# Step 0's order on TensorE, the keys' lower halves, and a block finished ahead of a maximum, in a fused attention and gated-mix block on one core

## The chip, the cores and the metric

One core of a Trainium2 chip runs the whole program; the other cores are idle. The time is the device time of one execution in microseconds. Before the change it is the median of three runs. One more execution was profiled, and all views below are of that one.

## What is computed

Inputs: `x` of 64 blocks with 256 rows and 512 columns, a context of the same shape, a 512 x 512 output weight with its bias, three 512 x 512 weights `W_r`, `W_k`, `W_v`, mixing vectors `mu_r`, `mu_k`, and two gates. All is float32. For each of the 64 blocks:

```python
q  = relu(layernorm(x)) per head (16 heads of 32)
k  = v = relu(ctx)      per head
att = softmax(q @ k.T / sqrt(32))            # 256 x 256 for each head
z  = relu((att @ v) @ ffn_w.T + ffn_b)
x1 = x + tanh(g_xattn) * z
xn = layernorm(x1); xp = xn shifted down by one row
r  = sigmoid((mu_r*xn + (1-mu_r)*xp) @ W_r)
kk = square(relu((mu_k*xn + (1-mu_k)*xp) @ W_k))
out = x1 + tanh(g_ffn) * r * (kk @ W_v)
```

## The kernel before

**A pipeline over the blocks.** `pipeline` (line 207) runs `iteration(i)` for i from -2 to 66; each of the five instruction streams (SP, POOL, ACT, VectorE, TensorE) has its own `iteration` with its own order written out by hand, and semaphores tie them together. No planner moves anything: every engine runs its list in order, and a wait holds all that stands behind it on that engine. The middle iterations are a hardware loop over pairs. In iteration i TensorE works on four blocks at once: the attention of block i, the first scores of block i + 1, the output projection of block i - 1, and the three products of the second half for block i - 2. The 16 steps of an iteration are separated by `shifted_scores(i, n)` for n from 0 to 15.

**Attention.** A product in high accuracy is three products of high and lower halves. Keys and queries are stacked instead: three groups of 32 rows (high, high, low halves) make one product with 96 rows. `scores(b, n)` (897) gives the scores of head n; `head_max` (692, VectorE) takes their maxima by rows; after four heads `turn_m` (879) transposes the maxima, `copy_m` (703) copies them to `m_t`, and `move_m` on SP's queue brings them as a 97th row beside the stacked queries. `shifted_scores` (910) makes the scores anew, transposed and with the maximum taken off; `exponent` on ACT makes `probs`. For each group of four heads c, `values(b, c)` (922) and `denominators(b, c)` multiply `probs` by the values and by ones, both in 32-column pieces into one bank. `norm_o(b, c)` (710, VectorE) divides. It waits for the denominators and for the landing of the previous group's `write_o`.

**From attention to the projection.** `write_o(b, c)` (282) puts a group, 128 KB, of `o_val` into DRAM, `read_o(b, u)` (288) reads two groups back transposed when both have landed; `o_high` on ACT (499) and `o_low` on POOL (359) split them, and `project(b, u, part)` (955) multiplies them with the weight. Its part 0 first puts the bias into the bank by a product with ones (line 960), then waits for `o_hi` and `o_lo`.

**The dense products.** `dense(q, part)` on TensorE stands for a quarter of one product into one bank: q 0 and 1 are `key` for block i - 2, 2 and 3 `project` for block i - 1, 4 and 5 `receptance`, 6 and 7 `value`, both for block i - 2. `finish(b, u)` (765, VectorE) waits for `value` and makes the output rows; its first instruction frees the bank that `dense(0, 0)` or `dense(1, 0)` of the next iteration takes.

**Transposes.** `turn(n)` takes the nth entry of a list of 14 transposes of queries, maxima or `xn`. All write one bank, so each waits until the one before is copied out.

**Keys.** SP loads `k_raw` of block i + 2 (`load_k`, 246) once block i + 1's keys are written. ACT makes the high halves (`k_halve`, 481), VectorE the lower ones in place (`k_low`, 679), SP writes both, 1 MB, to DRAM (`write_k`, 253), and `stack_k` (266) reads them back into the stacked form, one group of heads at a time. Before the change `k_halve(i + 2)` stands behind exponent 10, `k_low(i + 2)` is the last entry of VectorE's iteration behind `head_max(i + 1, 6)`, and `write_k(i + 2)` the last of SP's, behind `write_o(i, 2)`.

**Step 0 before.** On TensorE the order is `dense(0, 0)`, `scores(i, 7)`, `dense(0, 1)`, `shifted_scores(i, 1)`, `values(i - 1, 3)`, `turn(1)` (the maxima of heads 4 to 7), `denominators(i - 1, 3)`, `dense(0, 2)`. On VectorE it is `head_max(i, 7)`, `finish(i - 3, 1)`, `copy_m(i, 1)`, `norm_o(i - 1, 3)`, `mix_r(i - 2)`.

Of the kernel before, what the change touches and what calls it, by code (L numbers as in the profile page):

```python
# [16 lines left out]
def flamingo_block(nc, x, ctx_in, ctx_t, g_xattn, g_ffn, w_t, bias, mu, out):  # L17
# [30 lines left out]
    with es:  # L48
# [147 lines left out]
        def on(b):  # L196

            return not isinstance(b, int) or 0 <= b < NB
# [22 lines left out]
        def _(sp):  # L221
# [31 lines left out]
            def write_k(b, par):  # L253
                if on(b):
                    sp.wait_ge(k_hi_ready, b + 1)
                    sp.wait_ge(k_lo_ready, b + 1)
                    for half, tile in enumerate((k_high, k_raw)):
                        sp.dma_start(k_dram[par, :, half].rearrange("c f g t -> (f g) c t"),
                                     tile[:, :, :]).then_inc(k_written, 16)
# [22 lines left out]
            def write_o(b, c):  # L282
                if on(b):

                    sp.wait_ge(o_ready, CH * b + c + 1)
                    sp.dma_start(o_dram[c].rearrange("g f m r -> (g f) (m r)"), o_val[:, :]).then_inc(o_written, 16)

            def read_o(b, u):

                if on(b):  # L290

                    sp.wait_ge(o_written, 16 * (CH * b + 2 * u + 2))
                    for m in range(GR):
                        sp.dma_start(o_mv[HD * m:HD * m + HD, :, :],
                                     o_dram[2 * u:2 * u + 2, :, :, m, :].rearrange("c g f r -> f (c g) r")
                                     ).then_inc(o_moved, 16)

            def store(b, par):
                if on(b):
                    sp.wait_ge(out_ready, NU * (b + 1))  # L300
                    sp.dma_start(out[b].rearrange("(u p) d -> p u d", p=P), x1[:, par, :, :]).then_inc(stored, 16)

            def iteration(i, par):
                stack_k(i, 3, par)
                store(i - 3, 1 - par)
                move_m(i, 1)
                write_o(i - 1, 3)
                read_o(i - 1, 1)
                keys_written(i + 1)
                load_k(i + 2)  # L310
                stack_k(i + 1, 0, 1 - par)
                move_m(i, 2)
                write_o(i, 0)
                stack_k(i + 1, 1, 1 - par)
                load_x(i + 2)
                move_m(i, 3)
                write_o(i, 1)
                stack_k(i + 1, 2, 1 - par)
                move_m(i + 1, 0)
                load_w(i)  # L320
                read_o(i, 0)
                write_o(i, 2)
                write_k(i + 2, par)

            sp.dma_start(mu_sb[:, 0, :], mu[0]).then_inc(setup_loaded, 16)
            sp.dma_start(mu_sb[:, 1, :], mu[1]).then_inc(setup_loaded, 16)
# [102 lines left out]
        def _(act):  # L429
# [42 lines left out]
            def q_stack(b, c, u):  # L472
                if on(b):
                    act.wait_ge(q_turned, 2 * CH * b + 2 * c + u + 1)

                    after(act, st_ready, HEADS * (b - 1) + GR * c + GR)
                    nc.scalar.activation(q_st[0:QK, c, :, P * u:P * u + P],  # L477
                                         tp_bank[0:QK, :].rearrange("p (g t) -> p g t", g=GR),
                                         ACT.Copy).then_inc(q_stacked, 1)

            def k_halve(b):
                if on(b):
                    act.wait_ge(k_loaded, 16 * GR * (b + 1))
                    after(act, k_written, 32 * b)
                    nc.scalar.activation(k_high[:, :, :].bitcast(F32R), k_raw[:, :, :], ACT.Relu).then_inc(k_hi_ready, 1)
# [72 lines left out]
            def iteration(i, par):  # L558
                weights_split(i)
                q_stack(i, 2, 1)  # L560

                exponent(i, 0)

                exponent(i, 1)
                split_high(i, 0)
                q_stack(i, 3, 0)

                exponent(i, 2)
                split_high(i, 1)
                kt_relu(i - 2, 0)  # L570
                q_stack(i, 3, 1)
                split_high(i, 2)
                load_v(i, 1)
                q_high(i + 1, 0)
                split_high(i, 3)

                exponent(i, 3)

                exponent(i, 4)
                load_x1(i - 1, 1 - par)  # L580
                kt_relu(i - 2, 1)
                q_high(i + 1, 1)
                o_high(i - 1, 1)

                exponent(i, 5)
                split_high(i, 4)
                xr_high(i - 2)

                exponent(i, 6)
                split_high(i, 5)  # L590
                z_relu(i - 1, 0)
                q_stack(i + 1, 0, 0)

                exponent(i, 7)
                split_high(i, 6)
                q_stack(i + 1, 0, 1)

                exponent(i, 8)
                split_high(i, 7)
                ka_high(i - 2, 0)  # L600
                z_relu(i - 1, 1)
                q_stack(i + 1, 1, 0)
                ka_high(i - 2, 1)

                exponent(i, 9)
                xt_copy(i - 1, 0)

                exponent(i, 10)
                r_tanh(i - 2, 0)
                xt_copy(i - 1, 1)  # L610
                k_halve(i + 2)

                exponent(i, 11)
                q_stack(i + 1, 1, 1)

                exponent(i, 12)
                xk_high(i - 1, 0)
                r_tanh(i - 2, 1)

                exponent(i, 13)  # L620
                xk_high(i - 1, 1)
                q_stack(i + 1, 2, 0)

                exponent(i, 14)
                load_v(i + 1, 0)

                exponent(i, 15)
                o_high(i, 0)
# [5 lines left out]
        def _(dve):  # L634
# [57 lines left out]
            def head_max(b, n):  # L692
                if on(b):
                    dve.wait_ge(s_ready, HEADS * b + n + 1)
                    c = n // GR
                    if n % GR == 0:

                        after(dve, m_turned, CH * b + c - 1)
                    nc.vector.tensor_reduce(m_nat[:, c % 2, :, n % GR:n % GR + 1],  # L699
                                            s_bank[n % 2][:, :].rearrange("p (u y) -> p u y", u=NU),  # L700
                                            AX_X, ALU.max, negate=True).then_inc(s_maxed, 1)
# [72 lines left out]

            def iteration(i, par):

                head_max(i, 7)
                finish(i - 3, 1, 1 - par)
                copy_m(i, 1)
                norm_o(i - 1, 3)  # L780
                mix_r(i - 2)
                split_low(i, 0)

                head_max(i, 8)
                norm_1(i + 1)
                split_low(i, 1)

                head_max(i, 9)
                relu_v(i, 0)

                head_max(i, 10)
                split_low(i, 2)
                q_low(i + 1, 0)

                head_max(i, 11)
                split_low(i, 3)

                head_max(i, 12)
                split_low(i, 4)
                copy_m(i, 2)  # L800
                q_low(i + 1, 1)
                norm_o(i, 0)

                head_max(i, 13)
                relu_v(i, 1)

                head_max(i, 14)
                add_x(i - 1, 0, 1 - par)
                split_low(i, 5)
                split_low(i, 6)  # L810

                head_max(i, 15)
                norm_2(i - 1, 0, 1 - par)
                add_x(i - 1, 1, 1 - par)
                copy_m(i, 3)
                norm_2(i - 1, 1, 1 - par)

                head_max(i + 1, 0)
                split_low(i, 7)
                norm_o(i, 1)  # L820

                head_max(i + 1, 1)

                head_max(i + 1, 2)
                mix_k(i - 1)

                head_max(i + 1, 3)
                copy_m(i + 1, 0)

                head_max(i + 1, 4)  # L830
                stats_1(i + 2)
                finish(i - 2, 0, par)

                head_max(i + 1, 5)
                norm_o(i, 2)

                head_max(i + 1, 6)
                k_low(i + 2)

            dve.wait_ge(setup_act, 3)  # L840
            nc.vector.tensor_tensor(b_low, b_raw, b_rows[0:1, :].bitcast(F32), ALU.subtract).then_inc(setup_dve, 1)
# [6 lines left out]
        def _(pe):  # L848
# [163 lines left out]
            def iteration(i, par):  # L1012
# [40 lines left out]
                weights_split(i)  # L1053
                dense(0, 0)
                scores(i, 7)
                dense(0, 1)

                shifted_scores(i, 1)
                values(i - 1, 3)
                turn(1)  # L1060
                denominators(i - 1, 3)
                dense(0, 2)
                scores(i, 8)
                dense(0, 3)
# [126 lines left out]
```

## Time and profile before

| | us |
|---|---|
| median of three runs (lowest, highest) | 2936.23 (2931.65, 2940.18) |
| the profiled execution | 2935.97 |
| its span, first to last instruction | 2934.1 |
| TensorE busy | 2833.1 (97%) |
| VectorE busy | 2349.9 (80%) |
| ACT busy | 1568.1 (53%) |
| POOL busy | 1044.8 (36%) |
| TensorE idle in front of the product that waits for `o_lo` | 33.7 |

The mean clock granted to TensorE is 0.996 of full speed. The bytes moved are 408.56 MB, 139 GB/s over the span. To read it: TensorE is busy nearly all the time, so what matters is where its few waits stand, in which iteration, and who ends them. For this the orders in time of single engines are laid side by side. Times in them are microseconds from the start of the span; the iterations are alike, and one near 1000 us stands for them.

### The profile page before, as it was taken

To read this page: it belongs to the slowest core of one execution; us is meant where nothing else is said; L and a number is where in the kernel's file an instruction comes from. 1 tells how busy PE (TensorE), PEld (TensorE's weight loads), DVE (VectorE), ACT (ScalarE), POOL (GpSimd) and SP (SyncE) were. 2 spreads that over 40 slices of the span, in tenths; PEclk is the share of its full clock that TensorE was granted. 3 is DMA by queue.
4 is the path that set the end of the run, shared out by engine and by line. 5 is a ranking of instruction groups with operands and counts; after the bars stand their busy time and mean duration, and the time that the engine had idled before them with its cause. 6 is when DMAs were issued, how large, how long until landed. Compare 5 with 4: busy or idle time off the path is not lost. (4 is left out here: it accounts for less than half of the span.)

```text
span 2934.1 us, 71298 instructions
## 1 busy us (share of the span) xinstructions
PE 2833.1 (97%) x23168; PEld 2183.8 (74%) x23168; DVE 2349.9 (80%) x4175; ACT 1568.1 (53%) x2828; POOL 1044.8 (36%) x902
## 2 busy tenths in 40 slices
PE   3899999999999999999999999999999999999998
PEld 2677777777777777777777777777777777777776
DVE  5788888888888878878878878888888888888874
ACT  4455555555555555555555555555555555555552
POOL 0233333343343333333343333333333333333333
PEclk9999999999999999999999999999999999999999
DMA  5544545535445445445445445445445455355431
GB/s 167 153 129 145 154 121 151 155 121 154 151 123 156 143 127 159 138 130 159 138 131 159 133 138 155 129 145 153 126 147 156 121 152 154 122 154 149 126 104 42
DMA packets 405258, 408.56 MB, mean 139 GB/s; under 512 B 164577, under 2 KB 329441, under 8 KB 405218
## 3 DMA queue, kind: packets, MB, share of 16 engines
q1 hardware_dynamic: 352994, 340.92, 39.7%
q10 hardware_dynamic: 52224, 67.12, 7.0%
q8 instruction: 24, 0.39, 0.1%
q14 instruction: 16, 0.13, 0.0%
HBM read 272.64 MB, written 134.22 MB: 139 GB/s over the span
## 5 line engine op out<-in xcount | busy, mean ns | idle before, releaser
L699 DVE TENSOR_REDUCE m_nat<-bank 128x2 fp32r<-128x512 f32 x1024 | 694.6, 684 | 142.0 <-PE bank L906 141.5
L477 ACT ACTIVATE q_st<-bank 96x512 fp32r<-96x512 f32 x512 | 303.9, 593 | 765.7 <-PE bank L875 765.7
L496 ACT ACTIVATE probs<-bank 128x512 f32<-128x512 f32 x1024 | 593.6, 590 | 195.8 <-PE bank L918 187.2
L718 DVE RECIPROCAL o_val<-bank 128x256 f32<-128x256 f32 x256 | 449.3, 1755 | 60.4 <-PE bank L944 53.2
L918 PE MATMUL bank<-q_st,k_st 97*128 97x256 f32 x2048 | 437.9, 295 | 18.3 <-DMA q_st<-m_t 18.1
L906 PE MATMUL bank<-k_st,q_st 96*128 96x256 f32 x2048 | 430.0, 292 | 6.0 <-DMA k_st<-k_dram 4.5
L918 PEld LDWEIGHTS bank<-q_st,k_st 97*128 97x128 f32 x2048 | 345.5, 190 | 84.5 <-issue 22.6
L906 PEld LDWEIGHTS bank<-k_st,q_st 96*128 96x128 f32 x2048 | 356.8, 192 | 58.1 <-issue 5.9
L364 POOL TENSOR_TENSOR o_lo<-o_mv,o_hi 128x512 fp32r<-128x512 f32 x128 | 174.0, 1360 | 583.3 <-ACT o_hi L503 583.3
L397 POOL TENSOR_TENSOR xm<-xm 128x512 f32<-128x512 f32 x128 | 137.6, 1075 | 637.0 <-ACT xm L540 637.0
L708 DVE CAST m_t<-bank 4x256 fp32r<-4x256 f32 x256 | 105.1, 411 | 286.2 <-PE bank L884 286.1
L951 PE MATMUL bank<-xk_hi,w_hi 128*128 128x256 f32 x1024 | 298.3, 291 | 0.0
L951 PE MATMUL bank<-xk_lo,w_hi 128*128 128x256 f32 x1024 | 286.5, 280 | 0.0
L951 PE MATMUL bank<-xk_hi,w_lo 128*128 128x256 f32 x1024 | 286.5, 280 | 0.0
L932 PE MATMUL bank<-probs,v_pos 128*32 128x256 f32 x4096 | 275.8, 387 | 1.0 <-DVE o_val L720 1.0
L944 PE MATMUL bank<-probs,ones_r 128*32 128x256 f32 x4096 | 275.8, 387 | 0.0
L875 PEld LDWEIGHTS bank<-ident_r,q_nat 128*96 128x96 f32 x2048 | 192.6, 127 | 71.6 <-issue 52.5
L951 PE MATMUL bank<-w_hi,o_hi 128*128 128x512 f32 x512 | 212.0, 414 | 33.7 <-POOL o_lo L364 33.7
L875 PE MATMUL bank<-ident_r,q_nat 128*96 128x128 f32 x2048 | 218.4, 230 | 24.8 <-DVE q_nat L674 20.6
L382 POOL TENSOR_TENSOR xk_lo<-xm,xk_hi 128x512 fp32r<-128x512 f32 x128 | 165.1, 1290 | 216.1 <-ACT xk_hi L527 184.9
L951 PE MATMUL bank<-w_hi,xr_hi 128*128 128x512 f32 x512 | 208.0, 406 | 4.2 <-POOL xr_lo L390 4.2
L951 PEld LDWEIGHTS bank<-xk_hi,w_hi 128*128 128x128 f32 x1024 | 192.4, 188 | 26.0 <-issue 25.9
(90 smaller groups left out, 5893.6 us busy)
## 6 DMA issues: line engine op xcount, KB each, us to landing
k_st<-k_dram SPq DMA_DIRECT2D x256, 256.0 KB, 3.6
k_raw<-ctx_t_dram SPq DMA_DIRECT2D x256, 128.0 KB, 3.1
x_ln<-x_dram SPq DMA_DIRECT2D x256, 128.0 KB
k_dram<-k_high SPq DMA_DIRECT2D x64, 512.0 KB, 3.0
k_dram<-k_raw SPq DMA_DIRECT2D x64, 512.0 KB, 4.5
k_st<-k_dram SPq DMA_DIRECT2D x256, 128.0 KB, 3.5
o_dram<-o_val SPq DMA_DIRECT2D x256, 128.0 KB, 1.7
o_mv<-o_dram SPq DMA_DIRECT2D x512, 64.0 KB, 2.0
```

Of the source, the lines that this page charges most:

```text
L364: nc.gpsimd.tensor_tensor(by_tile(o_lo, u), o_mv[:, :, :].rearrange("p g (k a) -> p k g a", k=KC), by_tile(o_hi, u).bitcast(F32), ALU.subt ...
L382: nc.gpsimd.tensor_tensor(xk_lo[:, part, :], xm[:, part, :], xk_hi[:, part, :].bitcast(F32), ALU.subtract).then_inc(xk_lo_ready, 1)
L477: nc.scalar.activation(q_st[0:QK, c, :, P * u:P * u + P], tp_bank[0:QK, :].rearrange("p (g t) -> p g t", g=GR), ACT.Copy).then_inc(q_stack ...
L496: nc.scalar.activation(probs[:, n // GR % 2, n % GR, :, :].rearrange("p v t -> p (v t)"), st_bank[n % 2][:, :], ACT.Exp, scale=SCALE).then ...
L699: nc.vector.tensor_reduce(m_nat[:, c % 2, :, n % GR:n % GR + 1], s_bank[n % 2][:, :].rearrange("p (u y) -> p u y", u=NU), AX_X, ALU.max, n ...
L718: nc.vector.reciprocal(o_val[:, :], pv_bank[:, T:2 * T]).then_inc(rden_ready, 1)
L875: mm = nc.tensor.transpose(tp_bank[0:QK, P * g:P * g + P].bitcast(F32R), q_nat[:, u, GR * c + g, :, :], ident_r[:, :])
L906: mm = nc.tensor.matmul(s_bank[n % 2][:, T * u:T * u + T], q_st[0:QK, c, g, P * u:P * u + P], k_st[0:QK, c, g, :], start=True, stop=True)
L918: mm = nc.tensor.matmul(st_bank[n % 2][:, T * v:T * v + T], k_st[0:ST, c, g, P * v:P * v + P], q_st[0:ST, c, g, :], start=True, stop=True)
L932: nc.tensor.matmul(pv_bank[HD * g:HD * g + HD, 0:T], v_pos[:, v, HD * h:HD * h + HD], probs[:, c % 2, g, v, :], start=(v == 0), stop=(v == ...
L944: mm = nc.tensor.matmul(pv_bank[HD * g:HD * g + HD, T:2 * T], ones_r[:, 0:HD].bitcast(F32), moving, start=(n == 0), stop=(n == len(sums) - 1))
L951: mm = nc.tensor.matmul(dst, lhs[a], rhs[c], start=first and n == 0, stop=last and n == 2)
```

## The change

On TensorE, `values(i - 1, 3)`, `turn(1)` and `denominators(i - 1, 3)` move ahead of `dense(0, 1)` and `shifted_scores(i, 1)`. On VectorE, `finish(i - 3, 1)` moves ahead of `head_max(i, 7)`, and `k_low(i + 2)` moves from the end of the iteration to behind `head_max(i + 1, 1)`. On ACT, `k_halve(i + 2)` moves from step 10 to the end of step 7. On SP, `write_k(i + 2)` moves ahead of `write_o(i, 2)`. No instruction is added or removed.

```diff
@@ SP @@
                 read_o(i, 0)
+                write_k(i + 2, par)
                 write_o(i, 2)
-                write_k(i + 2, par)
@@ ACT @@
                 exponent(i, 7)
                 split_high(i, 6)
                 q_stack(i + 1, 0, 1)
+                k_halve(i + 2)
@@
                 exponent(i, 10)
                 r_tanh(i - 2, 0)
                 xt_copy(i - 1, 1)
-                k_halve(i + 2)
@@ VectorE @@
+                finish(i - 3, 1, 1 - par)
                 head_max(i, 7)
-                finish(i - 3, 1, 1 - par)
                 copy_m(i, 1)
@@
                 head_max(i + 1, 1)
+                k_low(i + 2)
@@
                 head_max(i + 1, 6)
-                k_low(i + 2)
@@ TensorE @@
                 dense(0, 0)
                 scores(i, 7)
-                dense(0, 1)
-
-                shifted_scores(i, 1)
                 values(i - 1, 3)
                 turn(1)
                 denominators(i - 1, 3)
+                dense(0, 1)
+
+                shifted_scores(i, 1)
                 dense(0, 2)
```

## Rows read from the trace of the kernel before

**Rows 1.** The page, busy time of each engine, share of the span, instructions.
```profile
PE 2833.1 (97%) x23168; PEld 2183.8 (74%) x23168; DVE 2349.9 (80%) x4175; ACT 1568.1 (53%) x2828; POOL 1044.8 (36%) x902
```

**Rows 2.** List of waits: who waited for whom, us in total, times, longest.
```profile
PE bank L951 <- POOL o_lo L364: 33.7, 62, 3.7
```

**Rows 3.** TensorE in order of time, step 0: start, us, what, count.
```profile
1013.52 0.40 PE L906 MATMUL bank<-k_st,q_st 96*128 96x256 f32 x2
1013.75 0.29 PE L951 MATMUL bank<-xk_hi,w_hi 128*128 128x256 f32 x1
...
1014.47 0.40 PE L918 MATMUL bank<-q_st,k_st 97*128 97x256 f32 x2
1014.80 1.07 PE L932 MATMUL bank<-probs,v_pos 128*32 128x256 f32 x16
1015.80 0.28 PE L884 MATMUL bank<-ident_r,m_nat 128*4 128x128 f32 x2
1016.01 1.07 PE L944 MATMUL bank<-probs,ones_r 128*32 128x256 f32 x16
```

**Rows 4.** VectorE in order of time, ahead of and in step 0.
```profile
1006.31 0.41 DVE L708 CAST m_t<-bank 4x256 fp32r<-4x256 f32 x1 [2.06 <-PE bank L884]
...
1013.63 1.22 DVE L682 SCALAR_TENSOR_TENSOR k_raw<-k_raw,k_high 128x1024 fp32r<-128x1024 f32 x1
1014.76 0.69 DVE L699 TENSOR_REDUCE m_nat<-bank 128x2 fp32r<-128x512 f32 x1
1015.36 0.68 DVE L769 SCALAR_TENSOR_TENSOR th<-th,bank 128x512 f32<-128x512 f32 x1
...
1016.74 0.41 DVE L708 CAST m_t<-bank 4x256 fp32r<-4x256 f32 x1
```

**Rows 5.** Turns of the maxima: one that waits (iteration 2), and two others.
```profile
126.93 0.69 DVE L699 TENSOR_REDUCE m_nat<-bank 128x2 fp32r<-128x512 f32 x1
...
127.67 0.28 PE L884 MATMUL bank<-ident_r,m_nat 128*4 128x128 f32 x2 [1.01 <-DVE m_nat L699]
...
172.28 0.28 PE L884 MATMUL bank<-ident_r,m_nat 128*4 128x128 f32 x2
...
2790.40 0.28 PE L884 MATMUL bank<-ident_r,m_nat 128*4 128x128 f32 x2
```

**Rows 6.** TensorE in order of time where the projection's second half begins.
```profile
1030.05 0.47 PE L960 MATMUL bank<-b_rows,ones_r 128*128 128x512 f32 x1
1031.11 0.47 PE L951 MATMUL bank<-w_hi,o_hi 128*128 128x512 f32 x1 [0.60 <-POOL o_lo L364]
1031.42 0.39 PE L951 MATMUL bank<-w_hi,o_lo 128*128 128x512 f32 x1
1031.64 0.39 PE L951 MATMUL bank<-w_lo,o_hi 128*128 128x512 f32 x1
```

**Rows 7.** ACT and POOL in order of time, the splits ahead of it.
```profile
1028.98 0.63 ACT L503 ACTIVATE o_hi<-o_mv 128x512 fp32r<-128x512 f32 x1 [2.83 <-DMA o_mv<-o_dram]
...
1029.68 1.28 POOL L364 TENSOR_TENSOR o_lo<-o_mv,o_hi 128x512 fp32r<-128x512 f32 x1 [3.46 <-ACT o_hi L503]
```

**Rows 8.** ACT and TensorE in order of time, the transposes' bank in step 9.
```profile
1037.01 0.59 ACT L477 ACTIVATE q_st<-bank 96x512 fp32r<-96x512 f32 x1
...
1039.21 0.66 PE L893 MATMUL bank<-ident_r,xn 128*128 128x128 f32 x4
```

**Rows 9.** The page, DMA issues: count, KB each, us to landing.
```profile
k_dram<-k_raw SPq DMA_DIRECT2D x64, 512.0 KB, 4.5
```

**Rows 10.** The start: ACT, VectorE, SP's queue and TensorE.
```profile
7.86 1.06 ACT L485 ACTIVATE k_high<-k_raw 128x1024 fp32r<-128x1024 f32 x1 [1.17 <-DMA k_raw<-ctx_t_dram]
...
14.46 1.29 DVE L652 BATCH_NORM_STATS2 st<-x_ln 128x6 f32<-128x512 f32 x2 [6.99 <-DMA x_ln<-x_dram]
...
17.45 0.43 SPq L258 DMA_DIRECT2D k_dram<-k_high  x1
...
28.55 1.20 PE L906 MATMUL bank<-k_st,q_st 96*128 96x256 f32 x4 [4.53 <-DMA k_st<-k_dram]
```

## The prediction

> **What bounds the kernel now.** I read the busy shares first, then the list of waits, then the order of time of single engines around step 0 of one iteration. TensorE is busy 97% of the span [rows 1]. In the steady stretch it waits for one thing alone: the product behind the bias row of `project(i - 1, 1)` waits for POOL's `o_lo` once in each iteration, 62 times and 33.7 us in all, of which 3.7 us is one wait near the end [rows 2]. So a busy TensorE sets the time, and an edit counts only if it adds or removes time in which TensorE stands still. Its own instructions are the same 23168 after the change, and all go to the same banks. Of the neighbours, the kinds of switch (scores to product, scores to 32-column values) are the same in number too: I cost the new order in itself at nothing.
>
> The o_lo wait ends a long chain that starts in step 0: `values(i - 1, 3)`, `denominators(i - 1, 3)`, `norm_o` on VectorE, `write_o` and `read_o` through SP's queue, `o_high` on ACT, `o_low` on POOL. `o_hi` starts at 1028.98, when the read lands, and `o_lo` runs from 1029.68 for 1.28 us [rows 7], and the product starts at 1031.11, with 0.60 us of idle [rows 6].
>
> **Step 0 on TensorE: a stall at the maxima's turn.** This is the largest new cost. Before, values start at 1014.80, the turn of the maxima at 1015.80 and the denominators at 1016.01 [rows 3]. The change puts `dense(0, 1)` and `shifted_scores(i, 1)` behind them. Together these fill from 1013.75 to 14.80. Values then follow scores(7), which start at 1013.52 and need about a third of a microsecond (14.47 to 14.80 is the same gap behind the other kind of scores), so at 1013.85; the turn would be free to start 1.00 later, at 1014.85 [rows 3].
>
> The turn needs `head_max(i, 7)`. On VectorE everything from `copy_m(i + 1, 0)` at 1006.31 to 1016.74 runs without idle. That copy is released by TensorE, so the chain hangs from the step before on TensorE itself and can't slide ahead. `k_low` starts at 1013.63, `head_max(i, 7)` at 1014.76 and is done at 1015.45; `finish` takes from 1015.36 to 1016.74, 1.38 us [rows 4]. The change takes `k_low` (1.13 us of VectorE) out of this chain and puts `finish` (1.38 us) in, ahead of the maximum. So `head_max(i, 7)` moves to 1013.63 + 1.38 = 1015.01 and ends at 1015.70, 0.25 later than now. `finish` itself waits for nothing there: `dense(7, 3)` is over before `dense(0, 0)`, and that is before 1013.5. A turn that waits for this maximum starts 0.05 us behind its end, in the stretch of the start where it does wait (126.93 + 0.69 = 127.62, then 127.67) [rows 5]. New turn: 1015.75. TensorE loses 1015.75 - 1014.85 = 0.90 us in each full iteration. It happens in the 60 full iterations whose turns run from 172.28 to 2790.40 us [rows 5], one in 44.37 us; the turn stands 0.35 us behind the maximum's end in the one shown (1015.80 and 1014.76 + 0.69), and I take it for all. 60 x 0.90 = 54 us. Bounds: 0.7 (if the gap behind scores is wider than I take it) to 1.05 (all that was moved behind).
>
> What queues behind the waiting turn: all of TensorE, so denominators (1015.96, hardly earlier than 1016.01), `dense(0, 1)`, `shifted_scores(i, 1)`, the exponents on ACT that feed on them. Thus the denominators, which the change was to bring forward, come 0.05 us earlier only, and the rest of the iteration comes 0.90 later.
>
> **What that buys at o_lo.** The wait at `project(i - 1, 1)` costs more than its idle time: from the bias row at 1030.05 to the product at 1031.11 are 1.06 us, where a product behind transposes comes 0.31 later, and the next one comes 0.31 behind it in place of 0.22 [rows 6]. That is 0.84 for 0.60 idle, so idle + 0.24. Without the tail's 3.7 and the first one in iteration 2, 60 waits hold about 29 us; 29 + 60 x 0.24 = 43 us. With TensorE 0.90 later at that point and a chain that is no later than now, the product would start at 1030.05 + 0.90 + 0.31 = 1031.26, and `o_lo` is there at about 1031.0 [rows 6, 7]: the wait is gone in the usual iteration without any help. There is help as well: today 1 MB of key writes goes onto SP's queue behind `k_low`, at about 1015, just ahead of this chain's traffic; now it leaves some 5 us earlier, and I expect `read_o` about 1 us earlier. So I take back all 43 us. Net of both: 54 - 43 = +11 us. The stall is not removed, it changes its place.
>
> **Keys: k_halve, k_low, write_k.** `k_low` goes between `head_max(i + 1, 1)` and `head_max(i + 1, 2)`. VectorE idles 2.06 us before `copy_m(i + 1, 0)` [rows 4], which is more than 1.13, so the copy stays in place: cost 0. It costs what exceeds that cover, 0.5 us an iteration if it were to take half a microsecond too much, since the whole chain to the turn hangs from this copy. Queued behind it are mix_k (and with it ACT's `xk_high`, 1.1 us later) with microseconds of room until `dense(0, 0)` of the next iteration. `k_halve` on ACT, about 1 us, at step 7 now, delays `z_relu`, `ka_high` and `q_stack(i + 1, 1, 0)`. The last is the tight one: its copy ends at 1037.60, so up to 1038.6 then, and the transposes that need its bank start at 1039.21 [rows 8]. Cost 0, with 0.6 us of room.
> `write_k(i + 2)` on SP now waits for keys that are long ready and goes right behind `read_o(i, 0)`, before `write_o(i, 2)`. What it can cost: `norm_o(i - 1, 3)` waits for `write_o(i - 1, 2)` to have landed. Key writes take 4.5 us to land [rows 9] from about 1010, so 1014.5 to 1015 and the small write behind them perhaps 1016; needed at 1017.3, when the denominators have ended (1016.01 + 1.07 [rows 3], and 0.2 to be seen). Cost 0, 1 us of room.
> The Trainium skill (DMA: Bandwidth & Descriptors, Queues, rings and completion order) says that a completion is counted only after every earlier write of the same DMA engine has landed, so the 128 KB write must outlast the megabyte ahead of it; no row of before has them in this order. By that rule the write is never faster than I took it here, and the sum is the same.
>
> **The start.** Before the loop is full, `k_low(0)` stands behind the layer-norm statistics, which wait 7 us for x until 14.46, though ACT had begun to halve the keys at 7.86; the key write goes out at 17.45 and the first scores, which wait for the stacked keys, start at 28.55 [rows 10]. With `k_low` first, the write can go at about 10.2. Upper bound 7.2 us earlier. But the queue is still busy with x until 14.46, so the write lands only some 3 to 4 us sooner; the lower bound is nothing. I take 4 us, since everything up to the first weights hangs from this, and 1 us more in iteration 1, where the turn already waited for VectorE and now has `k_low`'s 1.13 us less ahead of it. In iteration 2, at 127.67 [rows 5], the two sides cancel. The tail's chain, with the wait of 3.7, starts about 0.8 us earlier since `dense(0, 1)` no longer stands ahead of the last values. Together -6 us (0 to -10).
>
> **Sum.** The profiled run took 2935.97 us with a span of 2934.1, 0.3 under the median of 2936.23. 2936 + 54 - 43 - 6 = 2941 us.
>
> **Rivals.** (1) Both stalls stand: the turn costs 0.90 and o_lo still waits, because the queue's new order makes the read or the small write late by more than 0.3 us beyond TensorE's own lag (`write_o` past 1017.3, as above). 2936 + 54 - 6 = 2984. For it: the room at the landing is an estimate. Against: 2 of 3 terms of that chain lose traffic. 7 in 100. (2) A second place gives way, most likely the turn of the next maxima behind the moved `k_low`, or the bank behind `q_stack`: 0.3 to 0.5 us in each iteration, decided from 0.5 us of room: 2941 + 18 to 30 = 2959 to 2971. 15 in 100. (3) The turn doesn't stall, because the maximum comes early enough (VectorE's chain would have to lose 0.9 us) and only the o_lo wait falls: 2936 - 43 - 6 = 2887. Against: rows 4 leave no idle in the chain. 8 in 100. (4) As forecast, but with a loss of 0.7 at the turn and a better start: 2941 - 12 - 4 = 2925, 15 in 100. (5) The edit does nothing: the o_lo loss stays and the turn finds its maximum, 2936 less the start's 6, 2930: 5 in 100. The forecast has 50 in 100, with its own range 2930 to 2955.
>
> **How the numbers follow.** About 0.3% (9 us, so 2927 and 2945) is what a measurement can tell from none. Faster: (3), (4) and a little of the forecast, 0.25. Slower: (1), (2) and the forecast's upper part, 0.35. Same: 0.40. Range: 2918 to 2968, which leaves out (3), (1) and the end of (2).
>
> **What would show it.** Right: the wait of `project` for o_lo vanishes from the list and a wait of L884 for the maxima appears, about 60 times 0.8 to 0.9 us; denominators keep their distance to scores(7) plus 0.0 to 0.1; VectorE shows an idle gap ahead of `norm_o(i - 1, 3)`; the first scores start near 24.5. Wrong: no wait at L884 (then 2890 or so), waits at both (2984), or a new one at transposes L875/L893.

## The result, and the profile after

The changed kernel takes 2943.39 us (median of ten, 2941.84 to 2945.57), the kernel before 2936.07 (2931.65 to 2940.18). The ratio is 1.0026 with a 95% interval of 1.0018 to 1.0034: slower by about 7 us, a quarter of a percent. The forecast was 2941. The profiled execution has a span of 2940.1 us, 6.0 more than before, with 0.995 of the full clock.

The page's busy line, to be laid beside [rows 1]:

```profile
PE 2824.0 (96%) x23168; PEld 2184.4 (74%) x23168; DVE 2472.0 (84%) x4175; ACT 1568.8 (53%) x2828; POOL 1037.3 (35%) x902
```

TensorE has 9 us less of busy time in a span that is 6 longer. VectorE has 122 us more with the same 4175 instructions; that wasn't forecast, and its cause stands further down. The list of waits of TensorE (us in total, times, longest), of the whole run, answers to [rows 2]:

```profile
PE bank L884 <- DVE m_nat L699: 58.9, 63, 2.2
...
PE bank L951 <- POOL o_lo L364: 1.5, 2, 1.1
```

The wait for `o_lo` has gone from 33.7 us to 1.5. The turn of the maxima (line 884), which before waited five times, all of them at the start, now waits in each steady iteration. Step 0 of one iteration, TensorE and VectorE in order of time (start, us, what, idle before and who ended it), beside [rows 3, 4]:

```profile
1013.21 0.40 PE L906 MATMUL bank<-k_st,q_st 96*128 96x256 f32 x2
1013.54 1.07 PE L932 MATMUL bank<-probs,v_pos 128*32 128x256 f32 x16
1015.53 0.28 PE L884 MATMUL bank<-ident_r,m_nat 128*4 128x128 f32 x2 [0.92 <-DVE m_nat L699]
1015.74 1.07 PE L944 MATMUL bank<-probs,ones_r 128*32 128x256 f32 x16
```

```profile
1006.00 0.41 DVE L708 CAST m_t<-bank 4x256 fp32r<-4x256 f32 x1 [0.92 <-PE bank L884]
...
1013.33 0.68 DVE L769 SCALAR_TENSOR_TENSOR th<-th,bank 128x512 f32<-128x512 f32 x1
1014.04 0.75 DVE L772 SCALAR_TENSOR_TENSOR x<-th,tgh,x 128x512 f32<-128x512 f32 x1
1014.71 0.69 DVE L699 TENSOR_REDUCE m_nat<-bank 128x2 fp32r<-128x512 f32 x1
1015.96 0.41 DVE L708 CAST m_t<-bank 4x256 fp32r<-4x256 f32 x1 [0.56 <-PE bank L884]
```

Values start at 1013.54 and the turn could follow 1.0 us later. The maximum of head 7 stands behind `finish` and ends at 1015.40; the turn starts 0.13 behind it. It is 1.99 us behind the values' start here and in nearly every steady iteration, where it was 1.00 before. That is 0.98 us lost; the length of the iteration, beside the same kernel with the maximum first (e3 below), gives 44.65 - 43.68 = 0.97, for a forecast of 0.90.

The projection's second half, TensorE and POOL, beside [rows 6, 7]:

```profile
1030.74 0.47 PE L960 MATMUL bank<-b_rows,ones_r 128*128 128x512 f32 x1
1031.04 0.40 PE L951 MATMUL bank<-w_hi,o_hi 128*128 128x512 f32 x1
```

```profile
1027.41 1.29 POOL L364 TENSOR_TENSOR o_lo<-o_mv,o_hi 128x512 fp32r<-128x512 f32 x1 [0.51 <-ACT o_hi L503]
```

The product comes 0.30 us behind the bias row, with no wait. `o_lo` is ready at 1028.70, 2.3 us before it is wanted; before it came too late. SP's queue shows where the time of that chain has gone: the key write, the store of a finished block (`out_dram`), the last group's write and its read, and the fetch of `x` that ACT puts on its own queue. Before:

```profile
1014.92 0.39 SPq L258 DMA_DIRECT2D k_dram<-k_high  x1
...
1018.64 0.39 SPq L301 DMA_DIRECT2D out_dram<-x  x1
...
1019.94 0.37 SPq L286 DMA_DIRECT2D o_dram<-o_val  x1
1023.01 1.86 SPq L294 DMA_DIRECT2D o_mv<-o_dram  x4
...
1023.86 0.45 ACTq L453 DMA_DIRECT2D x<-x_dram  x1
```

After:

```profile
1009.20 0.39 SPq L258 DMA_DIRECT2D k_dram<-k_high  x1
...
1015.13 0.39 SPq L301 DMA_DIRECT2D out_dram<-x  x1
...
1019.33 0.34 SPq L286 DMA_DIRECT2D o_dram<-o_val  x1
1021.04 1.80 SPq L294 DMA_DIRECT2D o_mv<-o_dram  x4
...
1024.54 0.38 ACTq L453 DMA_DIRECT2D x<-x_dram  x1
```

From the write's issue to the read's are 1.71 us. Before the change they were 3.07. The list of DMA issues gives how long each took to land (KB, us). Before, the store, the group's write and the last piece of its read:

```profile
out_dram<-x SPq DMA_DIRECT2D x1, 512.0 KB, 4.0
...
o_dram<-o_val SPq DMA_DIRECT2D x1, 128.0 KB, 3.1
...
o_mv<-o_dram SPq DMA_DIRECT2D x1, 64.0 KB, 4.5
```

The megabyte of keys isn't itself in the way: its second half went out at 1015.35 and took 4.5 us, so it had landed at 1019.85, just before the group's write was issued. But SP stood at the key write until `k_low` was done, and what stands behind it in SP's list came late, the 512 KB store above all. The list of waits of SP has it, about 1.3 us an iteration before, and 2.2 us once in all of the changed kernel:

```profile
SPq L256 <- DVE k_raw L682: 89.6, 63, 9.3
```

The late key write cost the chain in two places. First, the store was issued 1.3 us ahead of the group's write and landed at 1022.69; the write was counted as landed 0.30 us later. In the steady iterations of the kernel before, e2, e5 and e7 this distance is 0.24 to 0.36 us, though the write takes from 2.0 to 4.8; where the store has landed in time, the write takes 1.70. Second, the read's third and fourth pieces went out at and behind the fetch of `x` and took 4.3 and 4.5 us, where the changed kernel's, ahead of it, took 2.1 and 2.3. Over the steady stretches of all 13 traces, 2807 pieces issued more than 0.3 us ahead of that fetch landed in 2.2 us (median; longest 3.6), 149 issued together with it or behind it in 4.1, and the 52 between in 3.6. Both are read from landing times: no run moved the store or the fetch by itself.

An iteration takes 44.65 us now, in all 57 steady ones within 0.02; before it took 44.37 on average, 44.27 in most. Laid side by side by the first bias row of each iteration, the changed kernel is 4.0 us ahead in iteration 2, 10.2 behind at the last one, 2890.82 against 2880.63, and 6.0 behind at the end. So the start gave 4, the loop took 14, and the tail gave 4. The last two intervals of the loop are short of the steady ones: 44.58 and 43.68 us, where they were 45.03 and 45.14 before, which is 1.9 us back.

### The profile page after: what moved, and what is told of

Same layout as the page of the kernel before. It is cut to its first block, busy times and chain, and to the rows that moved or that the text cites. A ratio compares the mean times of both kernels' runs of the same rounds, so it can differ in the third digit from the quotient of the medians.

```text
span 2940.1 us, 71356 instructions
## 1 busy us (share of the span) xinstructions
PE 2824.0 (96%) x23168; PEld 2184.4 (74%) x23168; DVE 2472.0 (84%) x4175; ACT 1568.8 (53%) x2828; POOL 1037.3 (35%) x902
## 4 chain that ended last, share of the span: by engine, by line
PE 76%; DVE 16%; issue 5%; DMA 1%; SPq 1%; DVEq 1%; POOL 0%; ACT 0%; POOLq 0%; ACTq 0%
PE bank L951 40%; PE bank L918 8%; PE bank L932 7%; PE bank L944 7%; PE bank L906 6%; DVE m_nat L699 5%; DVE o_val L718 4%; PE bank L875 3%; DVE th L769 3%; PE bank L893 2%; DVE st L652 2%; PE bank L884 2%; PE bank L960 1%; DVE mv L657 0%; DMA o_mv<-o_dram 0%
## 5 line engine op out<-in xcount | busy, mean ns | idle before, releaser
L397 POOL TENSOR_TENSOR xm<-xm 128x512 f32<-128x512 f32 x128 | 144.7, 1130 | 689.5 <-ACT xm L540 689.5
L364 POOL TENSOR_TENSOR o_lo<-o_mv,o_hi 128x512 fp32r<-128x512 f32 x128 | 164.8, 1287 | 371.2 <-ACT o_hi L503 371.2
L356 POOL TENSOR_TENSOR rstd<-ve,mhalf 128x1 f32<-128x1 f32 x128 | 69.2, 540 | 539.6 <-DVE ve L736 539.6
```

The costliest lines, as they stand in the source:

```text
L364: nc.gpsimd.tensor_tensor(by_tile(o_lo, u), o_mv[:, :, :].rearrange("p g (k a) -> p k g a", k=KC), by_tile(o_hi, u).bitcast(F32), ALU.subt ...
```

## The experiments

The theory, A: TensorE asks for the maximum 1 us sooner, VectorE delivers it 0.25 later since `finish` stands ahead, and the difference is the cost; the key moves free the `o_lo` chain, and TensorE's lag covers that as well. Rivals: the order on TensorE costs in itself; the moved `k_low` slows VectorE; the `o_lo` wait goes only because TensorE is late.

**The order on TensorE put back.**

```diff
+                dense(0, 1)
+
+                shifted_scores(i, 1)
                 values(i - 1, 3)
                 turn(1)
                 denominators(i - 1, 3)
-                dense(0, 1)
-
-                shifted_scores(i, 1)
```

> The changed kernel with TensorE's step 0 put back: dense(0, 1) and shifted_scores(i, 1) ahead of the last group's values again; all moves on VectorE, ACT and SP stay. Theory A (the 0.97 us at the maxima's turn is the cost, made by finish ahead of the maximum together with the earlier turn, and the o_lo wait is lifted by the key write's earlier place): the turn is wanted about 0.95 us later, when the maximum is just done, so its wait falls to 0 to 0.1 us; no o_lo wait comes back; 2943 - 60 x 0.9 = about 2888 us. Rival B (the o_lo wait was lifted only because TensorE arrives 0.97 us later): it returns with about 0.7 us an iteration, 2928 us. Rival C (the loss is VectorE slowed by the moved k_low, the order on TensorE is neutral): 2940 to 2945 us.

Measured: 2886.67 us beside 2934.55 for the kernel before, ratio 0.9833 (0.9816 to 0.9849). Between 200 and 2750 us no wait of TensorE is left in the list, neither kind; 43.68 us an iteration. Theory A holds to 1 us; rivals B and C are out. In the trace the turn stands 0.13 us behind the maximum's end and 1.03 to 1.05 behind the values' start in place of 1.00: it is just met.

**The order on TensorE alone**, in the kernel before, the same lines the other way.

> The kernel before with only TensorE's step 0 reordered as in the change. Theory A: the maximum of head 7, behind k_low as before, ends 0.25 us sooner than in the changed kernel, so the turn loses about 0.72 us an iteration; the o_lo chain gains 0.2 us and TensorE comes 0.7 later, so that wait mostly goes (-0.7). Net nearly nothing, 2936 to 2943 us, with a list of waits that has L884 at about 40 us and o_lo at under 12. Rival B' (o_lo wait stays as it is): 2936 + 43 = 2979 us. Rival C: no wait at L884, 2893 to 2936 us.

Measured: 2940.39 us, ratio 1.0015 (1.0005 to 1.0024), as theory A has it. The waits of TensorE between 200 and 2750 us:

```profile
PE bank L884 <- DVE m_nat L699: 37.8, 57, 0.7
PE bank L951 <- POOL o_lo L364: 5.0, 12, 1.1
```

A lag of about 0.7 us alone takes the `o_lo` wait from 57 iterations to 12. It works twice: TensorE comes later, and so does the fetch of `x`, 4.6 us behind the group's write in place of 3.9, so that as a rule only the last of the four pieces meets it. So either of the two is nearly enough to lift it, and in the full change they overlap. The order alone takes one wait for another of the same size.

**The maximum first.**

```diff
-                finish(i - 3, 1, 1 - par)
                 head_max(i, 7)
+                finish(i - 3, 1, 1 - par)
                 copy_m(i, 1)
```

> The changed kernel with one pair put back: head_max(i, 7) ahead of finish(i - 3, 1) on VectorE. Theory A: with k_low gone from the chain and finish behind, the maximum ends about 1.38 us sooner, 0.4 us ahead of the turn; no wait at L884, no o_lo wait: 2943 - 58 = 2885 us (44.65 to 43.68 us an iteration). Against: finish behind the maximum comes 0.6 us later and delays copy_m by that, which has microseconds of room. Rival C (k_low's new place costs VectorE's chain): a wait at L884 of 0.3 to 0.9 us stays, 2905 to 2943 us.

Measured: 2884.86 us, ratio 0.9829 (0.9812 to 0.9845). 43.68 us an iteration, no wait of TensorE between 200 and 2750. This is the changed kernel but for one pair of lines, and 58 us faster. It was timed once more, beside e10:

> e3's kernel once more, beside e10 and e11 on one chip: 2884 to 2886 us, so that e10's 1 to 3 us can be told from it.

Measured: 2886.17 us, ratio 0.9829 (0.9815 to 0.9842).

**The key moves alone**, both orders as before.

> The kernel before with only the key moves: k_halve at step 7, k_low behind head_max(i + 1, 1), write_k ahead of write_o; the pair on VectorE and the order on TensorE as before. Theory A: the turn is free, the read of the last group lands about 2 us sooner, the o_lo wait goes though TensorE arrives no later: 43.68 us an iteration, and the start and the tail gain 8 us as in the changed kernel: 2885 us. Rival B (the o_lo wait needed TensorE's lag): o_lo keeps 0.3 to 0.7 us an iteration, 2905 to 2928 us.

Measured: 2888.00 us, ratio 0.9838 (0.9822 to 0.9855). TensorE has no lag here, and the `o_lo` wait is gone all the same. The whole gain of the loop is in these moves. An iteration takes 43.645 us against 43.680 in the two kernels ahead of this one. In e1 the turn that is only just met comes 0.03 to 0.05 us late, which is enough. For e3 only the order on TensorE is left: 0.035 us an iteration, 2 us in all, which the forecast had at nothing. What e3 loses so it has back at the end (its `o_lo` wait in the tail is 1.46 us, e4's 3.44).

**finish ahead of the maximum, alone.**

```diff
+                finish(i - 3, 1, 1 - par)
                 head_max(i, 7)
-                finish(i - 3, 1, 1 - par)
```

> The kernel before with only finish(i - 3, 1) ahead of head_max(i, 7). Theory A (VectorE's chain from copy_m(i + 1, 0) to the maximum is a plain sum, and TensorE pays for what it exceeds): with k_low and finish both ahead, the maximum ends at 15.45 + 1.38 = 16.83 in the frame of rows 3 and 4, the turn starts 0.13 behind, 16.96, where it stood at 15.80: 1.16 us an iteration; denominators and the o_lo chain come as much later as TensorE, so that wait stays. 2936 + 60 x 1.16 = 3005 us. Rival D (finish is hidden, the 0.97 us of the changed kernel come from the order on TensorE): 2936 us.

Measured: 2964.62 us beside 2934.63, ratio 1.0100 (1.0083 to 1.0117). The half of theory A that is about the turn is right; its other half isn't. The turn, in this kernel's trace, and the waits between 200 and 2750 us:

```profile
1030.95 0.28 PE L884 MATMUL bank<-ident_r,m_nat 128*4 128x128 f32 x2 [1.11 <-DVE m_nat L699]
```

```profile
PE bank L884 <- DVE m_nat L699: 63.2, 57, 1.1
PE bank L951 <- POOL o_lo L364: 1.8, 2, 1.0
```

The turn comes 2.18 us behind the start of the values at 1028.77, so 1.18 lost, for 1.16 expected. But the `o_lo` wait has nearly gone, which is the 40 us to the 3005 expected. I had said that this chain slides with TensorE. It doesn't: the keys and the store go out as before while the group's write comes later. The store is 2.1 us ahead of it and not 1.3, so it takes 2.3 us (median) and not 3.1, and all four pieces of the read go out ahead of the fetch of `x`. `o_lo` starts 7.2 us behind the write's issue, where it was 9.5. The two waits that are left stand in iterations whose last pieces were issued behind the fetch.

**The key write last again**, in e4's kernel.

```diff
-                write_k(i + 2, par)
                 write_o(i, 2)
+                write_k(i + 2, par)
```

> e4's kernel (key moves alone) with write_k(i + 2) put back behind write_o(i, 2) on SP; k_halve and k_low stay early. The key write then goes out at about 13.2 in the frame of rows 3, between 9.2 (e4) and 14.9 (before). Theory E (o_lo's wait is lifted since the key write's megabyte no longer shares the queue with the last group's write and read): some wait may come back; 2888 to 2905 us. Theory F (any place ahead of stack_k(i, 3) will do, what counts is that SP isn't held by k_low): 2886 to 2889 us, no o_lo wait.

Measured: 2890.72 us, ratio 0.9850 (0.9834 to 0.9866); two waits for `o_lo`, 1.6 us in all, between 200 and 2750, again where the last pieces of the read follow the fetch of `x`. Nearly all of the relief comes from the keys being ready sooner. The place of `write_k` against `write_o` adds 0 to 3 us. The time doesn't tell theory E from F, but the landings speak against E as it was put: in the kernel before, the keys landed 0.04 us ahead of the issue of the group's write (median of the steady iterations), and the store, which stood between them, took 4.0 us there and 3.9 in the changed kernel. What the early `k_low` gives is that SP isn't held, so store and write are 2.2 us apart here and the group's write takes 2.1 us.

**The halving late again**, in e4's kernel: `k_halve(i + 2)` back to step 10 on ACT.

> e4's kernel with k_halve(i + 2) back behind step 10's xt_copy on ACT. By the forecast this move is hidden in both places: 2887 to 2889 us, the same iteration of 43.65 us. If k_halve at step 7 delayed the transposes' bank, this would be faster by up to 0.3 us an iteration, 2870 us; if its late place delays k_low, slower.

Measured: 2886.49 us, ratio 0.9836 (0.9820 to 0.9853), 43.64 us an iteration. The move on ACT is hidden in both places, as forecast. Its first bias row came 2.8 us sooner than in e4, so I tried the same in e3's kernel.

> e3's kernel (maximum first) with k_halve(i + 2) back behind step 10's xt_copy. The steady stretch has no wait to lose, so it stays at 43.68 us; what e8 gained over e4 was at the start, where the first bias row came 2.8 us sooner. If that adds here: 2881 to 2883 us; if it was chance: 2885 us.

Measured: 2885.64 us, ratio 0.9829 (0.9816 to 0.9843), not to be told from e12's 2886.17 on the same chip; its first bias row came at 90.36, e12's at 89.50. So the 2.8 us weren't the late halving; they look like chance.

**The change without its key moves**: both orders, `k_halve`, `k_low` and `write_k` where they were.

> The changed kernel without its key moves: TensorE's new order and finish ahead of the maximum, k_halve, k_low and write_k where they were. Theory A adds up: the maximum ends at 16.83, the turn starts at 16.96 where TensorE wants it at 14.86, 2.1 us an iteration; TensorE's lag lifts the o_lo wait (-0.7). 2936 + 60 x 2.1 - 43 = 3019 us, and no gain at the start. The keys' moves would then be worth 76 us in the changed kernel. Rival D (the costs of the order and of finish don't add): 2936 to 2985 us.

Measured: 3083.91 us, ratio 1.0510 (1.0492 to 1.0527), 65 us more than the sum. The turn waits 2.05 us in each iteration. One of four iterations lasts 45.76 us, which is just the sum (44.37 - 0.7 + 2.1); the other three last 47.3. What they add is TensorE's clock. The order of time behind one of these waits, and the windows over two such stretches (us, busy time of TensorE, its loads, VectorE, ACT, POOL with counts, then the granted clock):

```profile
1534.26 0.28 PE L884 MATMUL bank<-ident_r,m_nat 128*4 128x128 f32 x2 [2.05 <-DVE m_nat L699]
...
1536.59 0.41 PE L951 MATMUL bank<-xk_hi,w_hi 128*128 128x256 f32 x1
1536.80 0.41 PE L951 MATMUL bank<-xk_hi,w_lo 128*128 128x256 f32 x1
...
1539.11 0.28 PE L951 MATMUL bank<-xk_hi,w_lo 128*128 128x256 f32 x1
1539.23 0.28 PE L951 MATMUL bank<-xk_lo,w_hi 128*128 128x256 f32 x1
```

```profile
1534.00:1538.00 4.00, 3.74 (x28) 2.75 (x29) 2.40 (x4) 0.11 (x1) 0.00 (x0) 0.64 1.02 298
1582.00:1586.00 4.00, 4.00 (x31) 3.50 (x24) 3.28 (x6) 0.60 (x1) 0.00 (x0) 0.61 1.01 305
```

Products of one kind are 0.21 us apart at 1536.6 and 0.12 apart at 1539.1; the granted clock over those 4 us is 0.64 and 0.61, about three quarters of the time at the lower of its two levels, 1.2 GHz. In each of the long iterations the mean granted clock is 0.964, in each of the short ones 1.0. 45 such iterations of 1.5 us are 68 us, which is the 65 that were missing. Why one of four is spared is open. So the key moves are worth 140 us within the changed kernel, not 76, and 47 in the kernel before.

**The turn behind, all else early.**

```diff
                 values(i - 1, 3)
-                turn(1)
                 denominators(i - 1, 3)
                 dense(0, 1)
 
                 shifted_scores(i, 1)
+                turn(1)
```

> The changed kernel with one entry moved: turn(1) goes behind dense(0, 1) and shifted_scores(i, 1), values and denominators stay early. finish stays ahead of the maximum and the key moves stay. Theory A (TensorE pays only for asking for the maximum too early): the turn is then wanted 1 us later, at or behind the maximum, no wait at L884 in the steady stretch, 43.7 us an iteration, 2884 to 2888 us. Rival G (the 0.97 us come from values and denominators standing early, which the turn only shows): 2930 us or more.

Measured: 2919.66 us beside 2933.85, ratio 0.9950 (0.9935 to 0.9966), between the two. The turn doesn't wait, as theory A says, and the time still isn't 2886. The list between 200 and 2750 us names another place:

```profile
PE bank L906 <- DVE m_nat L699: 30.9, 58, 0.6
```

It is `scores(i, 10)`, which waits for the maximum of head 8. VectorE and POOL ahead of it:

```profile
1009.36 0.41 DVE L708 CAST m_t<-bank 4x256 fp32r<-4x256 f32 x1 [1.49 <-PE bank L884]
1009.70 1.75 DVE L718 RECIPROCAL o_val<-bank 128x256 f32<-128x256 f32 x1
...
1011.83 2.44 DVE L761 SCALAR_TENSOR_TENSOR xd<-xd,mu_sb,xt 128x256 f32<-128x256 f32 x4
1014.20 0.68 DVE L699 TENSOR_REDUCE m_nat<-bank 128x2 fp32r<-128x512 f32 x1
```

```profile
1012.92 1.07 POOL L397 TENSOR_TENSOR xm<-xm 128x512 f32<-128x512 f32 x1 [6.82 <-ACT xm L540]
```

`copy_m` waits 1.49 us for the later turn, and behind it stand `norm_o`, `mix_r` and the maximum of head 8. `mix_r`'s four instructions take 2.44 us here and 1.66 where POOL is idle. The first three take 0.48 us each; the fourth starts at 1013.01, while a square of POOL's runs from 1012.92, and ends at 1014.28, 0.28 behind it. Without those 0.8 us the maximum would be 0.2 us early. That `mix_r` is held by POOL is read from the overlap and wasn't tested by taking POOL's work away.

## Why the prediction was right

**What bounds the kernel.** Right. With all waits of TensorE gone, e1, e3 and e4 agree at 43.64 to 43.68 us an iteration; I had 44.37 - 0.7.

**The stall at the turn.** Right in place and cause, 0.07 short in size: 0.97 for 0.90. The term that was off is the step from the maximum's end to the turn. I took 0.05 us from the one stretch that shows it [rows 5]; in the steady stretch it is 0.13 in the changed kernel, e2, e5 and e9 alike. The row came from the start, where the engines' order was another, and it was the only one. With the key moves in, restoring either side (e1, e3) takes the stall away, so there it takes both the earlier request and the maximum behind `finish`. With `k_low` still ahead, either alone makes it: 0.73 us in e2, 1.18 in e5.

**What it buys at o_lo.** Right: 0.71 an iteration came back, of 0.72. I gave TensorE's lag as sufficient for the usual iteration and the queue as help. e2 and e4 show each by itself. The help was underrated, and it works otherwise than I said. I expected the read 1 us earlier, since the keys' megabyte would leave the queue just ahead of this chain. The read was issued 2.0 us earlier and `o_lo` came 2.3 us ahead of its need, because SP was no longer held, the store landed in time and the read went out ahead of the fetch of `x`. Neither the store nor the fetch stood in a term of mine.

**The order in itself at nothing.** Off by 0.035 us an iteration, 2 us.

**Keys.** The covers held. `copy_m(i + 1, 0)` still idles 0.92 us behind the moved `k_low`, the bank in step 9 wasn't late [rows 8], and `norm_o` waits for `write_o`'s landing only once, 2.0 us at the start (124.7). The keys took 5.8 us to land there and not 4.5: the second half went out at 1009.63 and landed at 1015.43, the small write behind it, issued at 1012.84, at 1015.72, 2.9 us later where 1.7 is usual. It was needed at 1016.8, so the room was 1.1 us. On the Trainium skill's rule on completions (DMA: Bandwidth & Descriptors, Queues, rings and completion order), the trace agrees: the small write was never counted before the megabyte ahead of it, but 0.17 to 1.0 us behind it in 57 steady iterations.

**Start and tail.** I had 4 + 1 for the start; it was 4.6 at the first scores and 4.0 at iteration 2. The rows that answer to [rows 10]:

```profile
10.36 0.43 SPq L258 DMA_DIRECT2D k_dram<-k_high  x1
...
23.95 1.20 PE L906 MATMUL bank<-k_st,q_st 96*128 96x256 f32 x4 [0.83 <-DMA k_st<-k_dram]
```

The tail gave 4, not 0.8. Its wait for `o_lo` shrank from 3.73 us to 1.12. That comes with TensorE's order: it is 1.26 and 1.46 in e2 and e3, which have the new one, and 3.4 to 3.6 in e1, e4 and e5, which haven't. With it went a loss that I hadn't counted: before, the products behind this wait ran at the lower clock. The kernel before, then the changed one:

```profile
2887.73 0.77 PE L951 MATMUL bank<-w_hi,o_hi 128*128 128x512 f32 x1 [3.73 <-POOL o_lo L364]
2888.30 0.63 PE L951 MATMUL bank<-w_hi,o_lo 128*128 128x512 f32 x1
2888.72 0.63 PE L951 MATMUL bank<-w_lo,o_hi 128*128 128x512 f32 x1
```

```profile
2895.35 0.47 PE L951 MATMUL bank<-w_hi,o_hi 128*128 128x512 f32 x1 [1.12 <-POOL o_lo L364]
2895.65 0.39 PE L951 MATMUL bank<-w_hi,o_lo 128*128 128x512 f32 x1
2895.88 0.40 PE L951 MATMUL bank<-w_lo,o_hi 128*128 128x512 f32 x1
```

They are 0.42 us apart in the one and 0.23 in the other; a dozen of them make about 2.3 us.

**The sum.** 58 at the turn, -43 at o_lo, +2 for the order, -4 at the start and -4 in the tail give +9, where the spans differ by 6 and the medians by 7; the last two iterations, 1.9 us better than the steady ones, are in none of these terms. The forecast was +5. The errors in the terms (4 at the turn, 2 for the order and 1 at the start on one side, 3 in the tail on the other) partly cancelled; a hit to 2 us of a sum of such terms is also luck.

**The rivals.** That both stalls stand, that a second place gives way and that no stall comes are all out by the lists of waits. A second place did give way, but only in e11, which is another order. The signs that I had named came: 0.92 us at the turn, the first scores at 23.95 for 24.5, and VectorE idle for 0.71 us ahead of `norm_o(i - 1, 3)`.

## What to carry to other kernels

On an engine that has no time to spare, an entry moved forward is worth nothing if what it needs isn't moved forward too: the same change with the maximum ahead of `finish` runs in 2885 us, 58 faster, and the difference is two lines on another engine. Before such a move, add up the in-order chain on the delivering engine from the last point that the waiting engine itself sets, and compare its end with the new time of need. And an issue that waits on an in-order queue holds all that stands behind it. The key write had time, but SP stood at it, and the store behind it went out just ahead of a small round trip that had none. Such a trip is checked by landing times, of its own queue and of the other engine's. The key moves, which took SP out of that wait, were worth more than any reordering of the products.

## What was not expected of the hardware

**A wait of 2 us costs clock.** Waits of 0.9 to 1.2 us in each iteration leave the granted clock at 0.995 to 0.996 (the changed kernel, e5). The one of 2.05 us in e9 brings it to 0.972, with 1.5 us more lost behind three of four waits. So the price of a stall isn't linear in its length: 1.2 us cost 1.2, 2.1 us cost 3.2 on average.

**VectorE beside POOL.** VectorE's 122 us more of busy time are mostly (94 us) one group, `q_low`, the second one of each iteration. It took 0.67 us:

```profile
1028.90 0.67 DVE L674 SCALAR_TENSOR_TENSOR q_nat<-x_ln,q_nat 128x512 fp32r<-128x512 f32 x1
```

Now, since `o_low` and with it `xr_low` run 2.3 us earlier on POOL and lie across it, it takes 2.24:

```profile
1029.59 2.24 DVE L674 SCALAR_TENSOR_TENSOR q_nat<-x_ln,q_nat 128x512 fp32r<-128x512 f32 x1
```

```profile
1028.90 2.38 POOL L390 TENSOR_TENSOR xr_lo<-xd,xr_hi 128x1024 fp32r<-128x1024 f32 x1 [0.20 <-issue]
```

It ends 0.55 us behind the end of POOL's instruction, which is about its own length. The Trainium skill (SBUF — State Buffer, SBUF: two separate sides) says that a VectorE instruction with two inputs in SBUF and a GpSimd instruction that reads SBUF exclude each other for the whole of whichever starts first. By that rule, the trace agrees: the held instruction ends about its own length behind POOL's, here (2.24 us for 0.67) and in e11 (the fourth of `mix_r`, 1.27 for 0.48). No run took POOL's instruction away. In the changed kernel the place has room for it; in e11 it hasn't, and TensorE stands still 0.53 us in each iteration.
